# Gated cross attention and ternary FFN on one core: the last block in two halves of 1024 columns, with 18 spare products on TensorE ahead of its down product

## The reference, cut to what matters

```python
x = x + tanh(g_xattn) * cross_attention(layernorm(x), ctx, ctx, mask)      # x: 4 x 2048 x 512
x = x + tanh(g_ffn) * ffn(layernorm(x))

def _act_quant(x):                                # per token: 127 / max|x|, round, scale back
    scale = 127.0 / clip(max(abs(x), axis=-1), 1e-05)
    return clip(round(x * scale), -128, 127) / scale

def ffn(x):                                       # weights rounded to -1, 0, 1
    gate = silu(bitlinear(x, w_gate))             # 512 -> 2048
    up = bitlinear(x, w_up)                       # 512 -> 2048
    return bitlinear(gate * up, w_down)           # 2048 -> 512, its input quantised by _act_quant
```

## Time and profile before

| | |
|---|---|
| median of 3 runs | 1346.26 us (1342.62 to 1346.9) |
| time of the profiled execution | 1347.23 us |
| its span, first to last instruction | 1345.4 us |
| TensorE products busy | 1253.8 us (93%) |
| VectorE busy | 1122.8 us (83%) |
| mean granted TensorE clock | 0.974 |
| last down product, first product to VectorE's start | 1335.75 to 1342.13 us |

### The profile page before, as it was taken

One profiled execution on the slowest core, in us unless ns is written; L12 is line 12 of the kernel. 1 busy time (PEld: TensorE's weight loads), 2 busy tenths in 40 slices (PEclk: granted clock), 3 DMA queues, 4 the chain that ended last, 5 costly groups with the idle time before them and its releaser, 6 DMA issues.

```text
span 1345.4 us, 26267 instructions
## 1 busy us (share of the span) xinstructions
PE 1253.8 (93%) x7552; PEld 620.8 (46%) x8126; DVE 1122.8 (83%) x2631; ACT 870.6 (65%) x1350; POOL 737.6 (55%) x1186
## 2 busy tenths in 40 slices
PE   4767699999999999999999999999999999999996
PEld 2223344445454454545454454545445454544542
DVE  6777597897979898897979899797979889796883
ACT  4886756658584766757575665757475665857562
POOL 2104654647475564657466564757566465747662
PEclk9867899999999999999999999999999999999998
DMA  9785348565665658564674756565574847565432
GB/s 327 234 253 114 72 80 172 115 151 115 130 138 111 146 117 169 114 147 113 122 158 89 172 117 150 116 143 124 109 155 109 179 106 152 113 133 98 87 83 67
DMA packets 386793, 181.64 MB, mean 135 GB/s; under 512 B 324323, under 2 KB 357987, under 8 KB 385123
## 3 DMA queue, kind: packets, MB, share of 16 engines
q1 hardware_dynamic: 386736, 181.04, 60.0%
HBM read 61.32 MB, written 35.46 MB: 72 GB/s over the span
## 4 chain that ended last, share of the span: by engine, by line
PE 52%; DVE 18%; DMA 12%; issue 6%; ACT 5%; SPq 4%; POOL 2%; POOLq 0%; ACTq 0%; DVEq 0%
PE bank L1247 16%; PE bank L1259 11%; PE bank L1107 6%; PE bank L1108 6%; PE bank L1109 6%; DMA aT<-ah 6%; PE bank L1186 4%; DVE nmax L987 4%; DVE region L1048 3%; DMA xT<-xh 2%; DVE ah L1011 2%; DVE hmx L1054 2%; POOL work L621 1%; DVE xn L972 1%; ACT work L744 1%
## 5 line engine op out<-in xcount | busy, mean ns | idle before, releaser
L630 POOL TENSOR_TENSOR region<-region,up 128x512 f32<-128x512 f32 x256 | 328.4, 1288 | 290.9 <-DVE region L1048 197.6
L1247 PE MATMUL bank<-tern_gate,region 128*128 128x512 fp8e4 x1024 | 264.6, 381 | 12.3 <-DMA region<-zb 9.3
L1247 PE MATMUL bank<-tern_up,region 128*128 128x512 fp8e4 x1024 | 263.7, 380 | 0.8 <-ACT up L783 0.8
L1259 PE MATMUL bank<-tern_down,region 128*128 128x512 fp8e4 x1024 | 234.5, 382 | 13.7 <-DMA region<-hb 9.6
L1048 DVE SCALAR_TENSOR_TENSOR region<-region,bank 128x512 f32<-128x512 f32 x256 | 170.5, 679 | 79.5 <-ACT region L775 79.2
L775 ACT ACTIVATE region<-bank,fs 128x512 f32<-128x512 f32 x256 | 176.5, 693 | 65.7 <-PE bank L1247 65.6
L621 POOL TENSOR_TENSOR work<-work 124x512 f16<-124x512 f32 x160 | 184.4, 1172 | 26.9 <-ACT work L744 19.9
L1054 DVE TENSOR_REDUCE hmx<-region 128x1 f32<-128x512 f32 x256 | 170.1, 675 | 27.0 <-POOL region L630 26.9
L783 ACT ACTIVATE up<-bank 128x512 f32<-128x512 f32 x256 | 153.9, 602 | 38.0 <-PE bank L1247 37.9
L788 ACT ACTIVATE hb<-region 128x2048 bf16<-128x2048 f32 x64 | 122.8, 1919 | 43.8 <-DVE region L1070 43.8
L1259 PEld LDWEIGHTS bank<-tern_down,region 128*128 128x128 bf16 x1024 | 97.8, 98 | 109.9 <-issue 3.5
(11 more groups left out here) (145 smaller groups left out, 2357.1 us busy)
## 6 DMA issues: line engine op xcount, KB each, us to landing
q_stack<-q_rows SPq DMA_DIRECT2D x96, 256.0 KB, 4.4
xbig<-in_x SPq DMA_DIRECT2D x16, 1024.0 KB, 5.3
q_rows<-q SPq DMA_DIRECT2D x64, 256.0 KB, 3.2
out_y<-o SPq DMA_DIRECT2D x64, 256.0 KB, 3.2
q_stack<-mT SPq DMA_DIRECT2D x32, 256.0 KB, 4.2
region<-in_wgT SPq DMA_DIRECT2D x4, 1024.0 KB, 9.5
region<-in_wuT SPq DMA_DIRECT2D x4, 1024.0 KB, 7.4
region<-in_wdT SPq DMA_DIRECT2D x4, 1024.0 KB, 6.0
```

The source lines that it names most:

```text
L630: nc.gpsimd.tensor_tensor(ht, ht, up[:, n % 2, :], ALU.mult).then_inc(hmul_ready, 1)
L1247: ins = T.matmul(pb[2 * (n % 2) + w][:, :], xqT[:, k, tok], tern[w][:, k * FF + n * GT:k * FF + (n + 1) * GT], start=(k == 0), stop=(k == ...
L1259: ins = T.matmul(pb[2][:, :], hT[:, t % 2, k, :], tern[2][:, k * GT:(k + 1) * GT], start=(k == 0), stop=(k == FK - 1))
```

## The change

Four steps of the last block are cut in two halves of 1024 columns, and nothing else of the program is cut. VectorE's `hq`, ScalarE's `h_integers` and SyncE's `h_transposed` each issue two instructions in place of one; the second transposing DMA reports to a semaphore of its own, `hT_last`. In `down`, TensorE starts when the first half has landed, and waits for `hT_last` and loads its weights again ahead of the ninth product. In addition, TensorE's table gets `I:hw69` twice ahead of `I:down30`: each is 9 products of 128x512 from `wq_hi` into bank 6, whose result nobody reads, and which wait for nothing.

```diff
+HALF = FF // 2
-    G:gu32 G:gu33 G:down20 I:down30
+    G:gu32 G:gu33 G:down20 I:hw69 I:hw69 I:down30
...
+        hT_last = sem("hT_last")
+        def final(f, t):
+            return isinstance(f, int) and f == NG - 1 and t == TT - 1
...
                 sp.wait_ge(hb_ready, f * TT + (t + 1))
                 if f * TT + t >= 2:
                     sp.wait_ge(down_mm, f * TT + (t - 1))
+                if final(f, t):
+                    for u in range(2):
+                        sp.wait_ge(hb_ready, f * TT + (t + 1) + u)
+                        sp.dma_start_transpose(hT[:, t % 2, u * FK // 2:(u + 1) * FK // 2, :],
+                                               hb[:, u * HALF:(u + 1) * HALF]).then_inc((hT_in[t % 2], hT_last)[u], 16)
+                    return
...
+                if final(f, t):
+                    for u in range(2):
+                        act.wait_ge(hq_ready, f * TT + (t + 1) + u)
+                        nc.scalar.activation(hb[:, u * HALF:(u + 1) * HALF], h[:, t % 2, u * HALF:(u + 1) * HALF],
+                                             ACT.Copy, bias=-MAGIC).then_inc(hb_ready, 1)
+                    return
...
+                if final(f, t):
+                    for u in range(2):
+                        V.tensor_scalar(h[:, t % 2, u * HALF:(u + 1) * HALF], h[:, t % 2, u * HALF:(u + 1) * HALF],
+                                        fs[:, t, HSC:HSC + 1], MAGIC, ALU.mult, ALU.add).then_inc(hq_ready, 1)
+                    return
...
+            def keep_warm(_, bank, n):
+                for k in range(n):
+                    T.matmul(pb[bank][:, :], wq_hi[:, 0, 0:P], wq_hi[:, 1, :], start=True, stop=True)
...
                 for k in range(FK):
+                    if final(f, t) and k == FK // 2:
+                        pe.wait_ge(hT_last, 16)
+                        T.ldweights(hT[:, t % 2, k, :], tile_position=(0, 0))
                     ins = T.matmul(pb[2][:, :], hT[:, t % 2, k, :], tern[2][:, k * GT:(k + 1) * GT], start=(k == 0), stop=(k == FK - 1))
```

More of the change, by code:

```diff
@@ L1263, in _ @@
                       "A": { "sc": scores, "pv": weighted, "wo": wo},
-                      "N": {}, "F": {"gu": gu, "down": down}}
+                      "N": {}, "F": {"gu": gu, "down": down, "hw": keep_warm}}
             pieces["W"] = {"km": keys_mm, "vm": values_mm}
```

## The result

The changed kernel takes 1340.78 us in the median of 8 runs (1339.54 to 1343.88), the one before 1345.05 us (8 runs, 1342.62 to 1346.9). The ratio is 0.9972 with a 95% interval of 0.9963 to 0.9981: 3.8 us less, between 2.6 and 5.0. (The two medians lie 4.27 us apart; the ratio weighs all 16 runs, and the text goes by it.) The profiled execution took 1339.75 us, its span is 1338.0 us.

What follows compares the result with a forecast made beforehand. TensorE bounds the whole program, the last block's chain of waits its end. Full clock (2.66 us) and earlier start (1.92) save 4.58; from the 1346.26 median that leaves 1341.68, and with 0.2 taken off the gain 1341.9 us, range 1340.0 to 1344.8.

Steps and rivals of the forecast that it cites:

- the tail: From the start of VectorE's rounding of the last block to the start of its last output; forecast 4.58 us shorter.
- VectorE and ScalarE: Last block's rounding and conversion in halves: roundings 1.50 us against 1.29, conversions ending at 1331.07 instead of 1331.37.
- SyncE: Its queue in the last block: both transposing DMAs stand behind tile 2's store, issued at 1330.67 and 1331.90.
- Landing: Each transposing DMA of 1024 columns lands 3.0 us after issue, bounds 2.1 and 3.2; halves there at 1333.67 and 1334.90.
- the bytes of the two touch: Bytes of tile 2's store and of the first transposing DMA overlap for about 0.1 us at most.
- Clock: TensorE's last product: spare products leave a 1.3 us gap, so it runs at full clock, saving 2.66 us; chance 0.78.
- The middle of the product: Ahead of TensorE's ninth product: second half is there 0.5 us early, so the wait there costs nothing.
- The fallen clock: Rival: TensorE's clock falls despite the spare products, last product slow as before, gain 1.92 us, 1344.3 us; chance 0.10.
- The rule on short idle spells: Skill page's claim on TensorE: short idle spells between groups of products can make the clock oscillate and cost throughput.
- The late half: Rival: the second transposing DMA takes 4.2 us, TensorE goes on 0.7 us late, gain 3.9 us, 1342.4 us; chance 0.06.
- the slower case: Rival: in SyncE's queue the second transposing DMA lands up to 13.7 us after issue, 1351.9 us; chance 0.03.
- The correction by 0.2 us: Taken off the gain because the clock may rise earlier in the old kernel's last product in other executions.

Runs made afterwards that it cites:

- e3: The changed kernel with the store of tile 2 moved behind the two transposing DMAs in SyncE's order; ratio to the kernel before 0.9957 (0.9943 to 0.9971).
- e1: The changed kernel with the halves but without the 18 spare products; ratio to the kernel before 0.9985 (0.9975 to 0.9994).
- e4: The kernel before with 32 spare products ahead of the undivided last block; ratio to the kernel before 0.9990 (0.9979 to 1.0001).
- e5: The changed kernel with 9 spare products in place of 18; ratio to the kernel before 0.9985 (0.9972 to 0.9997).
- e9: The kernel before, unchanged, profiled again without timed runs; tail 13.63 us.
- e10: The kernel before, unchanged, profiled once more without timed runs; tail 14.24 us.
- e11: The kernel before, unchanged, profiled a third more time without timed runs; tail 13.70 us.
- e7: The changed kernel with the store of tile 2 behind the transposes and the cut at 768 columns; ratio to the kernel before 0.9959 (0.9941 to 0.9977).
- e12: The changed kernel with the store of tile 2 behind the transposes and the cut at 896 columns; ratio to the kernel before 0.9963 (0.9950 to 0.9976).
- e2: The kernel before with 18 spare products ahead of the undivided last block, no halves; ratio to the kernel before 0.9983 (0.9971 to 0.9995).
- e8: The changed kernel with even halves and the store of tile 2 behind the transposes, run again; ratio to the kernel before 0.9967 (0.9952 to 0.9981).

## Why the prediction was right

The forecast was 1341.9 us and a gain of 4.4 us; measured were 1340.78 and 3.8 (2.6 to 5.0). The measured ratio lies 0.28% under 1, a hair inside the bound of 0.3% on whose other side I had put 0.52 of the chance; the interval straddles it. In absolute terms the forecast was 1.1 us too high, and the starting point explains that: I counted from 1346.26, the median of three runs of the kernel before, where eight have 1345.05. The gain itself was forecast in the tail as 4.58 and measured as 4.30.

- **VectorE and ScalarE.** The two roundings took 1.42 us where I had 1.50, the two conversions 2.01 where I had 2.11. The output of tile 2 began 1.33 us after the rounding's start, against a forecast of 1.41 and 1.20 before.
- **SyncE.** The step that looks small in the diff is the one that I would have missed without the queue's own rows. Transposes issued at +2.55 and about +3.9 after the rounding's start (forecast +2.53 and +3.76): behind the store, not when the data were ready. e3 showed it by moving the store.
- **Landing.** This is the term that was mis-sized: I took the best landing of its kind, 3.0 us, and the first took 3.33, the second 3.20, a little over the median of the earlier trace rows. TensorE followed the landing by 0.08 us where I had 0.16, and the issue was 0.02 late, so the first product began at +5.96 and not at +5.69. The tail came out 0.28 longer than forecast, 9.69 against 9.41, and 0.27 of it is this start. My bounds were 2.1 and 3.2, and it lies 0.13 outside. About half of the miss, 0.15 us, went when e3 moved the store away; I had seen that the bytes of the two touch for 0.1 us and had given it no price. That this meeting is what costs the 0.15 is not shown.
- **Clock.** Held at 1.00 through a gap of 1.6 us, product 3.63 us, VectorE 3.73 after its start, as forecast. e1 and e4 price the two parts alone: an earlier start by 1.63 to 1.65 us (forecast 1.92) and a shorter product by 2.65 us in the profiled pair (forecast 2.66), 2.56 against the mean of the four profiles of before. Against that mean, e1 gains 2.24 and e4 2.57 of the 4.20 us. These add up to more than the whole, because e1's product (5.67 us to the output) was shorter than those of before (6.29 in the mean). With the halves in place, the spare products are worth 11.65 - 9.69 = 1.96 us.
- **Luck in the clock.** I read from one profile that the clock falls after 2.3 us without a product. In the six profiles in which it fell before the last product or just as it began (before, e1, e5, e9, e10, e11), it did so 2.3 to 5.1 us after the product ahead. The profile that I had is the shortest of them; one like e11's would have let 9 spare products look enough, and e5 shows that they were not. That 1.6 us is safe in every execution is not shown: the change has one profile, and four more with 18 spare products and a cut block (gaps of 0.14 to 0.92) held too.
- **The middle of the product.** No stall, as forecast; e7 and e12 show how little cover there is: with the first piece two blocks smaller, 0.52 us open.
- **The rivals.** The fallen clock is real where the gap is longer: 3.24 us in e2 and 3.49 in e5. The rule on short idle spells, in "TensorE: Matmul & The Clock Gate", section "A second HAM failure mode: psum-queue depth-cycling", of the Trainium skill, did not show in this kernel: single gaps of 0.9 and 1.6 us left the clock at 1.00. It speaks of frequent spells, and no run here tests those. The late half and the slower case did not come: no piece of the cut block took more than 3.5 us to land.
- **The correction by 0.2 us** for the clock's rise in other executions had the right sign; four profiles make it 0.1.

The prediction knew a spread of 4.3 us among three runs, but not where it comes from: the front moves. The programs are the same up to the rounding, yet it began between 1324.70 us (e5) and 1328.90 (e11) in the 14 profiles. The first 200 us of the kernels before and after, and of e5:

```profile
0.00:200.00 200.00, 140.26 (x749) 66.10 (x773) 147.30 (x321) 134.32 (x168) 70.62 (x134) 0.85 0.66 180
```

```profile
0.00:200.00 200.00, 141.12 (x764) 67.42 (x788) 150.60 (x328) 137.04 (x172) 71.71 (x139) 0.87 0.67 183
```

```profile
0.00:200.00 200.00, 140.75 (x766) 66.82 (x790) 150.65 (x329) 136.99 (x173) 71.97 (x139) 0.88 0.67 184
```

The granted clock is 0.85, 0.87 and 0.88, and VectorE has started 321, 328 and 329 instructions at that point. Between 200 and 1300 us the clock is 1.00 in every profile. The same instruction of VectorE, its 321st, stands near the end of these 200 us before and after:

```profile
199.70 0.68 DVE L1038 TENSOR_REDUCE fs<-region 128x1 f32<-128x512 f32 x1
...
196.47 0.68 DVE L1055 TENSOR_REDUCE fs<-region 128x1 f32<-128x512 f32 x1
```

So the 3.1 us by which the front of the changed kernel was ahead of that of the profile before arose in the first 200 us, where nothing was changed: 3.23 us were there by then. That the clock's phases there cause it is argued, not shown: no run fixed them, and the mean clock alone doesn't order the profiles (0.86 in both e11 and e12, whose roundings began at 1328.90 and 1326.28).

## What to carry to other kernels

Where a program ends in a chain of waits, look at the granted clock of its last product: here 2.0 of the 4.2 us gained came from 18 products that nobody reads (the change against e1; 2.6 for the clock alone, in e4). They paid in full when they ended 1.6 us or less before the product could start, and not when they ended 3.2 us before it or delayed it; between 1.6 and 3.2 nothing was tried. A cut of a transfer in two is worth what the issuing queue lets it be: look first for what stands ahead of it in that queue, then place the cut so that the second piece arrives just as the first is used up. And a change of 0.3% in a kernel whose front scatters by 0.3% is judged better by a stretch of the trace that begins behind the scatter than by the runs, in more than one profile where that stretch varies too (13.63 to 14.24 us before).

## What the runs showed of the hardware that was not expected

- The clock can fall after TensorE has resumed: in e2 it was at 1.00 through 3.2 us without products and through the first 1.1 us of the next, and then 0.50 while the engine was working. In the profile before it had fallen after 2.3 us of idleness, in e1 after 2.7, in e5 after 3.5, and in e10, e9 and e11, which are the kernel before again, after 2.8, 5.0 and 5.1. A gap of a given length therefore doesn't decide alone. None of 1.6 us or less was seen to cost it: 1.60 us in the change, and in e8 a gap of 1.62 us that ended at 251.92, with a clock of 1.00.
- A transposing DMA of half the columns held SyncE for 1.23 to 1.33 us and landed after 3.1 to 3.3 (the change, e1, e3, e8), against 1.92 and 4.3 for the whole in the profile before: three quarters of the time for half of the bytes. The pieces of e7, 768 and 1280 columns, landed after 2.7 and 3.5.
- Two roundings of 1024 columns cost 0.13 us more than one of 2048 on VectorE, two conversions 0.10 more on ScalarE.
